# Cross attention on one core: weights, keys and values split into plain halves, and the folds of both heads of a pair put on separate halves of TensorE's rows

## The reference

```
qh = (x @ Wq + bq) in heads;  kh = (ctx @ Wk + bk);  vh = (ctx @ Wv + bv)
attn = einsum('bqhd,bkhd->hbqk', qh, kh) * mask;  attn -= max(attn)      # one maximum over everything
attn = exp(attn) * mask;  attn /= sum(attn over keys) + 1e-15
out = einsum('hbqk,bkhd->bqhd', attn, vh) @ Wo + bo + x
return (out - mean) / sqrt(var + 1e-5) * gamma + beta
```

## Time and profile before

| | |
|---|---|
| median of 3 runs | 1674.14 us |
| profiled execution | 1673.3 us, span 1671.5 us |
| TensorE busy | 1632.8 us, 98% |
| VectorE, ScalarE, GpSimd busy | 1149.0, 950.1, 445.6 us |
| granted TensorE clock, mean | 0.997 |

### The profile page before, as it was taken

How to read it: one execution, slowest core, us unless ns; L and a number is a source line. 1 busy time by engine, 2 the same in 40 slices (tenths; PEclk the granted TensorE clock), 3 DMA queues, 4 the chain that set the end, 5 groups by cost and what they waited for, 6 DMA issues and landing times. The chain is left out here.

```text
span 1671.5 us, 30882 instructions
## 1 busy us (share of the span) xinstructions
PE 1632.8 (98%) x11036; PEld 805.3 (48%) x11036; DVE 1149.0 (69%) x2247; ACT 950.1 (57%) x1418; POOL 445.6 (27%) x768
## 2 busy tenths in 40 slices
PE   4999999999999999999999999999999999999998
PEld 4545556465554554555644444444444444444443
DVE  7766555665565645655565888787787878888785
ACT  6866555555545555555555665566555665566541
POOL 0000000000000000000000366556655566556655
PEclk8999999999999999999999999999999999999999
DMA  7473455452735436335434766665565556665412
GB/s 239 152 265 123 152 189 169 163 194 75 263 100 206 173 123 232 126 148 191 164 127 167 305 235 244 252 226 208 220 243 207 207 220 226 251 232 204 179 64 76
DMA packets 81622, 315.18 MB, mean 189 GB/s; under 512 B 5409, under 2 KB 9761, under 8 KB 71841
## 3 DMA queue, kind: packets, MB, share of 16 engines
q1 hardware_dynamic: 81568, 314.47, 51.6%
HBM read 184.43 MB, written 130.02 MB: 188 GB/s over the span
## 5 line engine op out<-in xcount | busy, mean ns | idle before, releaser
L100 PE MATMUL ps_o<-u,p_hi 128*128 128x512 f16 x1024 | 388.8, 380 | 1.1 <-DMA u<-u_halves 0.8
L91 PE MATMUL ps_s<-x_hi,g_hi 128*128 128x512 f16 x1024 | 388.4, 379 | 0.0
L92 PE MATMUL ps_s<-x_lo,g_hi 128*128 128x512 f16 x1024 | 388.1, 379 | 0.0
L93 PE MATMUL ps_s<-x_hi,g_lo 128*128 128x512 f16 x1024 | 388.1, 379 | 0.0
L101 PE MATMUL ps_o<-u,p_hi 128*128 128x512 f16 x1024 | 388.1, 379 | 0.0
L102 PE MATMUL ps_o<-u,p_lo 128*128 128x512 f16 x1024 | 388.1, 379 | 0.0
L554 ACT ACTIVATE s<-ps_s,c_bias 128x512 f32<-128x512 f32 x256 | 176.2, 688 | 304.8 <-PE ps_s L93 301.6
L690 DVE TENSOR_TENSOR score_max<-score_max,tile_max 128x1 f32<-128x1 f32 x257 | 40.6, 158 | 306.3 <-ACT s L554 304.5
L761 POOL PARTITION_ALL_REDUCE key_max<-early_max x1 | 0.7, 715 | 881.8 <-DVE early_max L699 881.8
L1341 POOL TENSOR_TENSOR y<-y,gamma_b 128x512 f32<-128x512 f32 x124 | 157.8, 1273 | 232.5 <-ACT y L1072 232.5
L1059 ACT ACTIVATE p_hi<-ps_bc 128x512 f16<-128x512 f32 x256 | 151.4, 594 | 86.3 <-DVE ps_bc L1207 86.2
(11 more groups left out here) (123 smaller groups left out, 2373.2 us busy)
## 6 DMA issues: line engine op xcount, KB each, us to landing
scores<-s SPq DMA_DIRECT2D x30, 2048.0 KB, 7.6
x<-xT_in SPq DMA_DIRECT2D x32, 1024.0 KB, 9.3
u_halves<-u_out SPq DMA_DIRECT2D x64, 512.0 KB, 3.4
u<-u_halves SPq DMA_DIRECT2D x16, 2048.0 KB, 7.7
s_more<-scores SPq DMA_DIRECT2D x16, 2048.0 KB, 7.9
y<-x_in SPq DMA_DIRECT2D x32, 1024.0 KB, 9.9
out<-y SPq DMA_DIRECT2D x31, 1024.0 KB, 4.3
s<-scores SPq DMA_DIRECT2D x14, 2048.0 KB, 7.7
```

What stands on the lines that cost most here:

```text
L91: pe.matmul(out, lhs_hi, rhs_hi, start=first, stop=False)
L92: pe.matmul(out, lhs_hi, rhs_lo, start=False, stop=False)
L93: return pe.matmul(out, lhs_lo, rhs_hi, start=False, stop=last)
L100: pe.matmul(out, lhs_hi, rhs_hi, start=False, stop=False, skip_group_check=True)
```

## The change

- Weights: `wq_hi`, `wq_lo`, `wo_hi`, `wo_lo` lie plainly, high and low each in an array of its own, head 0 on rows 0 to 63 and head 1 on rows 64 to 127. One instruction a chunk on ScalarE and one on VectorE.
- Keys and values: `kv_hi` and `kv_lo` of one plain form, one instruction each; `v_lo` and the memset are gone. The host swaps the two heads in pairs 4 to 7 of the values' and output weights.
- Query fold: 24 matmuls of 64 rows x 128 columns, the two heads alternating, each head into its own bank. It waits for both banks at once. Two of the later four folds stand ahead of score tile 1 and two ahead of tile 3, on all engines. In the first pass each two folds wait for their own weights.
- Bias: 8 matmuls of 64 rows a group, each head in a bank of its own; VectorE scales, adds and turns them in eight small instructions (two before).
- Quad: 24 matmuls of 64 x 64, two tiles' four quarters at a time. Its waits stand ahead of the last three matmuls of the score tile in front.

```
-            for i in (2 * p, 2 * p + 1):
-                    dp = i % 2
-                    pe.wait_ge(f_lo_done, g * FT + i + 1)
-                    tile = ps_f[i % GBANKS][:, :].rearrange("r (j b h k) -> r j b h k", j=2, b=GB, h=2)
-                    for j in range(2):
-                        cols = slice((2 * dp + j) * P, (2 * dp + j + 1) * P)
+                pe.wait_ge(f_lo_done, g * FT + 2 * p + 2)
+                tiles = [ps_f[(2 * p + h) % GBANKS] for h in range(2)]
+                for c in range(DC):
+                    cols = slice(c * P, (c + 1) * P)
+                    for k, (weights, keys) in enumerate(((wq_hi, kv_hi), (wq_lo, kv_hi), (wq_hi, kv_lo))):
                         for h in range(2):
-                            for k, half in enumerate((kv_hi, kv_lo)):
-                                mm = pe.matmul(tile[:, j, :, h, :], wq2[:, p, h, cols], half[:, p, :, h, :],
-                                               start=(k == 0), stop=(k == 1))
-                    mm.then_inc(f_summed, 1)
+                            mm = pe.matmul(tiles[h][:, cols], weights[rows_of(h), p, cols], keys[rows_of(h), p, :],
+                                           start=(k == 0), stop=(k == 2), skip_group_check=True)
+                mm.then_inc(f_summed, 2)
...
+def fold_head_outputs(pe, banks, v, w, tiles):
+    (v_hi, v_lo), (w_hi, w_lo) = v, w
+    for two in (0, 2):
+        for k, (values, weights) in enumerate(((v_hi, w_hi), (v_hi, w_lo), (v_lo, w_hi))):
+            for bank, (p, b) in zip(banks[two:two + 2], tiles[two:two + 2]):
+                for h in range(2):
+                    rows = rows_of_values(p, h)
+                    mm = pe.matmul(bank[rows_of(h), :], values[rows, p, b * NK:(b + 1) * NK], weights[rows, p, :],
+                                   start=(k == 0), stop=(k == 2), skip_group_check=True)
...
                 for p in pairs:
+                    for k, half in enumerate((kv_hi, kv_lo)):
+                        for h in range(2):
+                            mm = pe.matmul(ps_k[h][:, 2 * p:2 * p + 2], half[rows_of(h), p, :], bq2[rows_of(h), p, :],
+                                           start=(k == 0), stop=(k == 1), skip_group_check=True)
...
-                    if u == 0 and p < NP - EARLY:
-                        fold_q(g, EARLY + p)
+                    if u == 0 and p in (1, 3):
+                        fold_q(g, EARLY + p - 1, first)
+                        fold_q(g, EARLY + p, first)
...
                     for c in range(DC):
+                        if c == DC - 1 and p in quad_behind[u]:
+                            before_quad(g, quad_behind[u][p], first)
...
             kv_out(0, 0)
-            round_kv(0, K_SCALE, False)
-            round_kv(0, K_SCALE, True)
+            round_kv(0, K_SCALE)
             round_x(0, 0)
...
+                for h in range(2):      # VectorE, bias(g)
+                    parts = ps_k[h][:, 0:2 * NP].rearrange("r (p k) -> r p k", k=2)
+                    dve.tensor_scalar(c_parts[:, h, :], parts[:, :, 0], 1 / (W_SCALE * K_SCALE), None, ALU.mult)\
+                       .then_inc(c_parts_done, 1)
...
```

More of the change, by code:

```diff
@@ L118, in rows_of, with rows_of_values @@
     return slice(h * DK, (h + 1) * DK)
[L121 to L133, removed]
+def rows_of_values(p, h):
+    return rows_of(1 - h if p >= NP // 2 else h)
 def place(p):
     return 2 * (p % (NP // 2)) + p // (NP // 2)
[L142 to L153, removed]
+def fold_head_outputs(pe, banks, v, w, tiles):
[7 more added lines that the diff above has]
+                                   start=(k == 0), stop=(k == 2), skip_group_check=True)
     return mm
@@ L181, in scores_phase @@
         kv32 = sb("kv32", [P, NP, KC])
[L182 to L183 removed]
+        kv_hi, kv_lo = sb("kv_hi", [P, NP, KC], F16), sb("kv_lo", [P, NP, KC], F16)
         x32 = sb("x32", [P, 2, DC, TT])
@@ L235, in weight_parts @@
                 hi, lo = (wk_hi, wk_lo) if i < 4 else (wv_hi, wv_lo)
[L236 to L242, removed]
+                return hi[:, c, :], lo[:, c, :], w32_i
+            hi, lo = (wq_hi, wq_lo) if i < 8 else (wo_hi, wo_lo)
+            return (*(w[:, 2 * c:2 * c + 2, :].rearrange("r p d -> r (p d)") for w in (hi, lo)), w32_i)
         def staging(i):
@@ L387, in bias, with fold_q @@
                 if p == NP - 1:
                     mm.then_inc(c_summed, 1)
[L390 removed]
+            def fold_q(g, p, first):
                 if p == 0:
[L393 to L406 removed]
@@ L418, in fold_o @@
-                fold_head_outputs(pe, [ps_f[(f + j) % GBANKS] for j in range(QU)], kv_hi, v_lo, wo2,
+                pe.wait_ge(f_lo_done, u_tile(g, q, 0)[0] + QU)
+            def fold_o(g, q):
+                _, f = u_tile(g, q, 0)
+                fold_head_outputs(pe, [ps_f[(f + j) % GBANKS] for j in range(QU)], (kv_hi, kv_lo), (wo_hi, wo_lo),
                                   [(q + j % 2 * (NP // 2), j // 2) for j in range(QU)]).then_inc(f_summed, QU)
@@ L469, in _, with split_weight @@
             act.sem_inc(s_out, SBANKS)
-            def split_weight(i, halves=(0, 1)):
+            def split_weight(i):
                 act.wait_ge(*w_loaded(i))
[L473 to L479, removed]
+                hi, _, w = weight_parts(i)
+                act.activation(hi, w, ACT.Copy, scale=W_SCALE).then_inc(w_hi_done, 1)
             def split_ctx(g):
@@ L502, in kv_out, with round_kv @@
                                    bias=bkv[:, half, p:p + 1], scale=1 / (W_SCALE * CTX_SCALE)).then_inc(kv32_done, 1)
[L504 to L511, removed]
+            def round_kv(i, scale):
+                act.wait_ge(kv32_done, NP * (i + 1))
+                act.activation(kv_hi[:, :, :], kv32[:, :, :], ACT.Copy, scale=scale).then_inc(kv_hi_done, 1)
             def round_g(g, p):
@@ L549, in scores_out @@
                 for p in range(NP):
-                    if u == 0 and p < NP - EARLY:
+                    if u == 0 and p in (1, 3):
+                        round_g(g, EARLY + p - 1)
                         round_g(g, EARLY + p)
                     act.wait_ge(s_summed, n * NP + p + 1 + 2 * NP)
-                    k = GB * p + u // UB
-                    act.activation(s32[:, u % 2, p, :], ps_s[p % SBANKS][:, :], ACT.Identity, bias=c_bias[:, k:k + 1],
+                    act.activation(s32[:, u % 2, p, :], ps_s[p % SBANKS][:, :], ACT.Identity, bias=c_bias[:, p, u // UB:u // UB + 1],
                                    scale=1 / (G_SCALE * X_SCALE)).then_inc(s_out, 1)
[L556 to L559, removed]
+                    if u == 1 and p == 0:
+                        round_kv(2 * g + 1, V_SCALE)
+                    if u == 3 and p == 0 and not last:
+                        round_kv(2 * g + 2, K_SCALE)
                     if u == 1 and p == 3 and not last:
@@ L563, in scores_out @@
                         round_x(g, u + 1)
-                    if first and u == 2 and p == 0:
-                        split_weight(15, (0,))
                     if first and u < 3 and p in split_behind[u]:
-                        split_weight(split_behind[u][p], (1,) if split_behind[u][p] == 15 else (0, 1))
+                        split_weight(split_behind[u][p])
                     if first and u == 3 and p in (3, 5):
@@ L591, in _ @@
             act.wait_ge(small_in, 48)
-            for h in range(2):
-                act.activation(bq2[rows_of(h), :, h], bq32[rows_of(h), :], ACT.Copy, scale=W_SCALE)\
-                   .then_inc(bq_done, 1)
+            act.activation(bq2[:, :, 0], bq32[:, :], ACT.Copy, scale=W_SCALE).then_inc(bq_done, 1)
             for i in range(8):
@@ L620, in split_weight @@
                 dve.wait_ge(w_hi_done, i + 1)
-                for hi, lo, w in weight_parts(i):
-                    split = dve.scalar_tensor_tensor(lo, w, W_SCALE, lo if high_elsewhere(i) else hi, ALU.mult, ALU.subtract)
-                split.then_inc(w_lo_done, 1)
+                hi, lo, w = weight_parts(i)
+                dve.scalar_tensor_tensor(lo, w, W_SCALE, hi, ALU.mult, ALU.subtract).then_inc(w_lo_done, 1)
             def split_ctx(g):
@@ L1379 @@
                     part[32 * q + row] = (-1.0 if k >= 1 else 0.0, -1.0 if k >= 2 else 0.0)
+    heads = np.arange(HD).reshape(NP, 2, DK)
+    heads[NP // 2:] = heads[NP // 2:, ::-1]
+    heads = heads.reshape(HD)
     turned = np.roll(np.arange(B), -1)
```

109 lines of the change are left out of this document (50 added, 59 removed).

## The result

The changed kernel takes 1665.45 us (median of 4 runs, 1661.28 to 1666.15) against 1673.76 for the kernel before (now 4 runs): a ratio of 0.9946, 95% interval [0.9935, 0.9958]. A second set of 5 runs gave 1662.72 (1661.29 to 1663.11) against 1673.30: 0.9935 [0.9921, 0.9948]. The forecast was 1663.4 in 1659 to 1670. The profiled execution took 1665.72 us, 7.6 less than the one of before; 7.4 of it are gained by the last copy of scores (891.59 instead of 898.99 us).

What follows compares the result with a forecast made beforehand. TensorE, busy 1632.8 of 1671.5 us, was taken as the bound. Folds 1.9, quads 4.2, first-pass wait 0.3 and start 4.3 sum to 10.7 us: 1673.3 - 10.7 + 0.84 = 1663.4 us, range 1659 to 1670.

Steps and rivals of the forecast that it cites:

- Folds overlap at 56 ns a round: Query folds: the two heads' 64x128 matmuls run together, 12 rounds of 56 ns, 0.67 us a fold instead of 0.90.
- A change of shape costs 0.09 us: TensorE: each change into or out of row halves costs 0.09 us extra, six a pass for the folds, 0.54 us.
- rival B: Query folds: a change of shape costs 0.18 us, or a round takes 62 to 66 ns; 1667.5 us, chance 0.20.
- Most of the folds' matmul time is lost to the wait for VectorE: Query folds: of 1.8 us a pass, half lies under VectorE's splits and 0.6 pays shape changes; 0.27 us gained.
- Quads, 0.13 us each: Value folds: same six rounds, one change of shape less, 0.13 us a quad, four quads in eight passes, 4.2 us.
- the wait for weights in the first pass: First pass, quad 2: its wait for weights goes, with one split instead of four halves; 0.3 us.
- Undisturbed passes of 107.9: Scores phase: a loop pass over two batch rows lasts 107.9 us instead of 108.7.
- The start, 4.3 us: First pass: fewer weight and key instructions, x_hi 4.0 us earlier, fourth score tile at 45.5 instead of 49.81; 4.3 us.
- c_bias later, at no cost: VectorE's eight small bias instructions make c_bias about 1.5 us later; TensorE loses nothing, with 2 us of cover.
- A: Query folds: the heads' matmuls or weight loads take turns, 112 ns a round; 1694.6 us, chance 0.09.
- C: The start gains nothing and 24 quarter loads eat the quads' gain; 1672.2 us, chance 0.05.
- The rule of 107 ns a load: Page rule on query-fold weight loads: 128 columns cost 107 ns whatever the rows, 1.28 us a fold, some 1692 us total.

Runs made afterwards that it cites:

- Heads in turn: The changed kernel with each query fold's 24 matmuls ordered as twelve of head 0, then twelve of head 1: 1681.5 us in a single run.
- two folds ahead and its passes written out: The changed kernel with the next pass's folds 0 and 1 moved behind the last unit's score tile 3, and TensorE's passes 1 to 6 unrolled: 1650.50 us.
- undoing the start: The changed kernel with query-weight splits and first key roundings again in half-height instructions, as before the change, in time only: 1669.90 us.
- the folds one by one: The changed kernel with the later four query folds one each ahead of score tiles 0 to 3, instead of two and two: 1671.90 us.
- the kernel before with a pause: The kernel before with each pass's third fold waiting for three free banks instead of one, making one long pause: 1680.19 us.

## Why the prediction held, point by point

1. *Folds overlap at 56 ns a round.* Right: 0.68 us a fold. Heads in turn, 2.3 us a pass longer, show what it is worth.
2. *A change of shape costs 0.09 us.* Right (0.31 instead of 0.216), also into row halves, against rival B.
3. *Most of the folds' matmul time is lost to the wait for VectorE.* Right, third fold 1.3 us late; the kernel with two folds ahead and its passes written out shows the price of that wait and of the fourth fold's, 1.7 us a pass (107.98 less 106.27). The fourth score tile comes 16.10 us after the last score matmul, before 16.46 (158.77 - 142.31): 0.36 gained, not 0.27, because the bias matmuls pair up. Only the group behind fold 3 counts, 0.1 us, as the others lie under the waits; the pairing I had only as an edge of the range. (The prediction's 15.98 and 16.25 count from 142.52, 0.21 us behind that matmul.)
4. *Quads, 0.13 us each.* Measured 0.12, with no round slowed by the 24 loads; the wait for weights in the first pass went.
5. *Undisturbed passes of 107.9.* Measured 107.98, 0.85 less than before. The forecast had 0.8.
6. *The start, 4.3 us.* Measured 5.5, and 0.9 of it is not what I had priced: the keys' projections end 0.9 us earlier than in the kernel before. Their first matmul starts at 13.19 instead of 13.71, as the weights landed earlier (ScalarE's first split of query weights at 12.10, not 12.62), and they last 0.4 us less. Both are luck of this pair of executions: in the traces here that matmul starts anywhere from 12.74 to 13.93, and from it to the last one it takes 6.7 to 7.9 us, in kernels with either start. The 4.6 left are near the forecast, and undoing the start costs 4.9.
7. *c_bias later, at no cost.* Right: ScalarE waits for it (its copy starts at 144.30), TensorE never.

The sum of these is 5.5 + 6.2 + 0.5 = 12.2 us, against 10.7 forecast, and 1673.4 less 12.2 is 1661.2: what a run without falls would take. The fastest run took 1661.28; that it had no falls is likely, but it was not traced. The weak step is the clock: I took the granted clock to matter only at the start and gave passes none of it. Three falls of 1.6 us took 4.8 back in the profiled execution, and the median was 1665.45 instead of 1663.4 (1662.72 in the second set, whose trace has one fall). That the medians lie so near the forecast is partly luck: two errors of opposite sign, the start and the bias too small, the falls left out. Rivals A and C did not happen, and B's 0.18 us for a change of shape was 0.09. Half-height loads of 128 columns keep 56 ns a round, two at a time; a load's own record lasts 94 ns, but the records overlap. The rule of 107 ns a load (the Trainium skill, TensorE: Matmul & The Clock Gate, LDWEIGHTS), taken as the pace of a fold, does not hold here.

Open: what decides in which pass a fall stands. Of the traces with a pause of 1.2 us and more ahead of the third fold three have falls in passes 2, 3 and 7, one has a fall in pass 5, and those of the folds one by one and of the kernel before with a pause have none. The pauses within a trace are alike, 1.2 to 1.5 us, with a fall behind them or without. Every fall seen in a pass begins 0.6 to 1.9 us behind the end of a pause or a stop, and no trace without one has a fall. So the pause goes with the falls, but that it causes them is argued, not shown.

## What to carry to other kernels

When a faster step only reaches the next wait sooner, move the step, not the wait: here TensorE waited 1.7 us a pass for VectorE's low parts of G until two folds were put ahead under score tiles. Alternate instructions between row halves one by one, as an engine that is given twelve of one half and then twelve of the other overlaps only three. And when a loop body grows, look at the instruction queue's packets: once the body is fetched again in every pass, dense short instructions behind the loop's jump can stop for it, and writing the passes out is the cure.

## What the runs showed of the hardware, unexpected

- A loop body of 800 matmuls a pass is not fetched again (33 instruction packets in all, none between 240 and 790 us); one of 896 is (80 packets, nine of 16 KB a pass), whether the 96 more are half-height or not. Where matmuls start every 28 ns behind the jump, TensorE stopped for 1.6 to 1.9 us in each looped pass, and nothing was lost where the passes were written out.
- Eight 64-row matmuls of 2 columns take 0.10 us in pairs, 25 ns a round, the pace of single full-height ones.
- The second execution of one kernel need not have its clock falls where the first had them: one trace has three falls and the other one, of 1.6 us each, and the two executions differ by 2.6 us.
